# Embedding gathers of chunks 1 to 3: a wait ahead of every two gathers in place of every eight

## The chip, the core and the metric

The kernel runs on one core of a Trainium2 chip. The time is device microseconds (us) of that core for one launch, lower is better. Everything is float32. The engines are TensorE (PE; its weight loads are shown apart as PEld), VectorE (DVE), ScalarE (ACT), GpSimd (POOL) and the queue engine SyncE (SP).

## What is computed

A recommendation tower over a batch of 2048. For each of 32 fields one row of 64 numbers is looked up in that field's own table; for every pair of fields a bilinear product with a 64x64 kernel gives one number; the 496 numbers go through a small network.

```python
e = jnp.stack([tbl_0[ids[:, 0]], ..., tbl_31[ids[:, 31]]], axis=1)   # (2048, 32, 64)
rows, cols = np.triu_indices(32, k=1)                                # 496 pairs
p, q = e[:, rows, :], e[:, cols, :]
pij = jnp.einsum('bpe,dpe,bpd->bp', p, kernel, q)
z = pij @ W.T + b
h = jnp.concatenate([z, dense_ctx], axis=1)
h = jnp.maximum(h @ W_top1 + b_top1, 0.0)
h = jnp.maximum(h @ W_top2 + b_top2, 0.0)
y = h @ W_top3
```

## The kernel before

The batch is cut into 4 chunks of 4 tiles of 128 rows (512 samples). Two fields lie side by side on the 128 partitions and are called a double; there are 16, numbered j = 0 to 15.

**Gathers.** GpSimd fetches the table rows with indirect DMAs, one for each field and tile: 128 rows of 64 floats, 32 KB. A double of one chunk is 2 fields x 4 tiles = 8 gathers. Doubles 3 to 6 go into `emb_first`, which has a buffer for odd and one for even chunks; the others go into `emb`, which has one. For chunk 0 the gathers are issued as early as their order allows (the first six fields are not gathered there but looked up by matmuls). For chunks 1 to 3 they are issued while the chunk before is worked on, and paced: ahead of the 8 gathers of a double stands one wait on `s_bilinear`, the count of slots that TensorE has finished. Its threshold is 40 + 4.6 x ((i - 1) x 16 + j) for chunk i and double j. A wait on the buffer's last reader stands there too (`turned(i - 1, j)`, or the batches of two chunks before).

**Turning.** For chunks 1 to 3 SyncE writes a gathered double of `emb` to HBM and reads it back so that 32x32 blocks lie where VectorE's block transpose (`turn_squares`, L675) can finish the turn into `emb_t`. Doubles 3 to 6 are turned by TensorE (`turn`, L745) and copied by ScalarE. The doubles 0 to 2 of the next chunk are turned at slots 80 to 84 of a chunk's 92, those in `emb_first` at slots 86 and 90, doubles 7 to 15 at slots 8 to 58 of their own chunk.

**Pairs.** A slot (`slot`, L773) multiplies one double with the kernels of another double on TensorE, in 32-column tiles of the array: 8 matmul calls, 16 MATMUL instructions. VectorE multiplies the result in PSUM with the other double (`multiply`, L654). 32 batches a chunk (`batch`, L787) do the same with the operands' roles changed; VectorE multiplies (L665) and ScalarE sums along the row (`reduce`, L584). The products of the slots are summed over partitions by more matmuls (`sum_quad`, L816), the sums of the batches join them (`join`, L799), and the network's layers (`layer_terms`, L859) follow. The results of slots and batches stand in a ring of three pairs of PSUM banks: TensorE can be three units ahead of VectorE.

**Order.** The order of all steps is fixed ahead, in the list `PROGRAM`, that TensorE, VectorE and ScalarE walk through; semaphores tie them. GpSimd has its own loop over chunks and doubles; so has SyncE.

Of the kernel before, what the change touches and what calls it, by code (L numbers as in the profile page):

```python
# [17 lines left out]
DOUBLES = NUM_FIELDS // 2  # L18
# [87 lines left out]

GATHER_LEAD, LEAD_FROM = 3, 7
GATHER_FROM, GATHER_EVERY = 40, 4.6

# [176 lines left out]
def build(nc, moved, tables, ids, looked_ids, dense_t, k_slots, w_cols, l0_b, w_top1, b_top1, w_top2, b_top2, w_top3, out):  # L288
# [6 lines left out]
    with ExitStack() as ctx:  # L295
# [6 lines left out]
        def sem(name):  # L302
            return ctx.enter_context(nc.semaphore(name))
# [64 lines left out]
        s_bilinear = sem("s_bilinear")  # L368
# [15 lines left out]
        def gathered(i, j):  # L384

            if j in BATCH_DOUBLES:
                return (s_gathered_first[i % 2][BATCH_DOUBLES.index(j)],
                        sum(32 * tiles for _, tiles in CHUNKS[i % 2:i + 1:2]))
            first = CHUNKS[1][0] if j < LOOKED_UP else 0
            return s_gathered[OTHER_DOUBLES.index(j)], 32 * (CHUNKS[i][0] + CHUNKS[i][1] - first)  # L390
# [10 lines left out]
        def turned(i, j):  # L401

            if i == 0 and j < LOOKED_UP:
                return s_looked_up, (j + 1) * TABLE_STEPS
            if i > 0 and j not in BATCH_DOUBLES:
                return s_squares, SQUARES_USE[i, j] + 1
            return s_turned, TURN_OF[i, j] - LOOKED_UP + 1

        def fields_of(i, j, t):

            if j in BATCH_DOUBLES:
                at = 2 * BATCH_DOUBLES.index(j)
                return emb_first[:, i % 2, t, at:at + 2, :]
            return emb[:, OTHER_DOUBLES.index(j), t, :, :]
# [58 lines left out]
        @block.gpsimd  # L473
        def _(pool):
            nc.gpsimd.iota(rows_i32[:], pattern=[[1, TABLE_STEPS]], base=0,
                           channel_multiplier=TABLE_STEPS).then_inc(s_rows, 1)
            pool.wait_ge(s_ids[0], 16)
            for i, (start, tiles) in enumerate(CHUNKS):
                if i == 1:
                    pool.wait_ge(s_consts, 1)  # L480
                    pool.wait_ge(s_ids[1], 16)

                    pool.wait_ge(s_one_hot, LOOKED_UP * TABLE_STEPS)
                for j in range(LOOKED_UP if i == 0 else 0, DOUBLES):
                    if i > 0:
                        pool.wait_ge(s_bilinear, int(GATHER_FROM + GATHER_EVERY * ((i - 1) * DOUBLES + j)))
                    elif j >= LEAD_FROM:
                        pool.wait_ge(*turned(0, j - GATHER_LEAD))
                    if j not in BATCH_DOUBLES:

                        if i > (1 if j < LOOKED_UP else 0):
                            pool.wait_ge(*turned(i - 1, j))
                    elif i > 1:

                        pool.wait_ge(*turned(i - 2, j))
                        pool.wait_ge(s_batch_prod, BATCHES_TO[i - 1])
                    for f in (2 * j, 2 * j + 1):
                        for t in range(tiles):
                            nc.gpsimd.indirect_dma_start(  # L499
                                fields_of(i, j, t)[:, f % 2, :], None, tables[f],  # L500
                                bass.IndirectOffsetOnAxis(ap=ids_sb[:, start + t, f:f + 1].bitcast(u32), axis=0),
                            ).then_inc(gathered(i, j)[0], 16)
                    if i == 0 and j == LOOKED_UP:
                        pool.wait_ge(s_consts, 1)
                        nc.gpsimd.affine_select(out=ident[:], in_=ident[:], compare_op=ALU.not_equal, fill=1.0,
                                                base=0, pattern=[[-1, P]], channel_multiplier=1).then_inc(s_ident, 1)
# [427 lines left out]
```

## Time and profile before

| | |
|---|---|
| median of 3 runs | 1318.49 us (1302.54 to 1324.91) |
| profiled execution, its own time | 1308.94 us |
| its span, first to last instruction | 1307.1 us |
| mean granted TensorE clock | 0.867 |
| TensorE matmul busy | 1155.0 us (88%), 11668 instructions |
| VectorE busy | 655.4 us (50%) |
| ScalarE busy | 547.3 us (42%) |
| GpSimd busy | 462.6 us (35%), 488 gathers |
| DMA mean | 38 GB/s |

Busy time counts a matmul from its start to a modelled end, and matmuls overlap: eight 32-column tiles run side by side. So the busy share of TensorE says little; how many MATMUL instructions are done in a microsecond says more. A window view counts an instruction in each window that it touches, so that in windows of 1 us, with matmuls of some 0.6 us, each is counted more than once; over 10 us and more that matters little. PEclk is the granted clock as a share of the full 2.4 GHz.

### The profile page before, as it was taken

The page shows a single profiled execution, that of the slowest core. Times are in us where ns is not written, and L with a number is a line of the kernel's source. Part 1 is how long each engine was busy: PE and PEld are TensorE (multiplying, and loading weights), DVE is VectorE, ACT ScalarE, POOL GpSimd, SP SyncE. Part 2 cuts the span into 40 slices and gives each one's busy share as a digit, 9 for nine tenths or more (in the row PEclk, how much of TensorE's full clock was granted, in tenths as well). Part 3 has the DMA queues.
Part 4 walks back from the last instruction along what each step waited for, and adds up shares of the span by engine and source line. Part 5 has one row for each costly group of instructions (what it writes and reads, how often), then busy time and mean ns, then how long its engine had stood idle before and what let it go on. Part 6 is the DMA issues. An engine that isn't in the chain of part 4 may idle for free.

```text
span 1307.1 us, 29606 instructions
## 1 busy us (share of the span) xinstructions
PE 1155.0 (88%) x11668; PEld 402.8 (31%) x11668; DVE 655.4 (50%) x620; ACT 547.3 (42%) x4163; POOL 462.6 (35%) x494
## 2 busy tenths in 40 slices
PE   5796999679998899998989898998888999999998
PEld 1231423022333224323333232333222333333333
DVE  3261746033445425454444443454444559769990
ACT  0000646124434213543435520235453455469991
POOL 6326242734344444433444444343444420000000
PEclk9796989568778798987779888988988879999999
DMA  7501000220022122012112002200321000400000
GB/s 234 200 11 23 11 17 10 50 40 17 12 49 49 25 58 49 17 28 48 34 41 41 17 18 59 51 16 16 74 57 34 15 12 3 83 2 3 3 3 2
DMA packets 115263, 50.04 MB, mean 38 GB/s; under 512 B 85362, under 2 KB 104562, under 8 KB 114612
## 3 DMA queue, kind: packets, MB, share of 16 engines
q1 hardware_dynamic: 97048, 28.99, 9.2%
q0 software_dynamic: 15616, 16.02, 6.3%
q10 hardware_dynamic: 2460, 3.15, 0.8%
q8 instruction: 91, 1.49, 0.5%
q14 instruction: 48, 0.39, 0.1%
HBM read 38.67 MB, written 9.45 MB: 37 GB/s over the span
## 4 chain that ended last, share of the span: by engine, by line
PE 80%; issue 11%; DVE 6%; another core or an unknown queue 1%; DMA 1%; ACT 0%; DVEq 0%; SPq 0%
PE bilinear L773 39%; PE sums L816 16%; PE bilinear L787 13%; PE bilinear L859 7%; PE bilinear L700 3%; DVE prod L654 3%; PE sums L799 1%; DVE prod L651 1%; DVE batch_prod L665 1%; PE bilinear L745 1%; DMA sums_sb<-looked_ids 1%; DVE w_comb_sb L634 1%; DVE emb_t L675 0%; PE bilinear L710 0%
## 5 line engine op out<-in xcount | busy, mean ns | idle before, releaser
L773 PE MATMUL bilinear<-emb_t,k_sb 64*32 64x512 f32 x5888 | 681.8, 654 | 59.5 <-issue 48.8
L584 ACT ACTIVATE batch_prod<-batch_prod 128x64 f32<-128x64 f32 x2048 | 490.8, 243 | 383.5 <-DVE batch_prod L665 311.9
L654 DVE TENSOR_TENSOR prod<-bilinear,emb_t 128x1024 f32<-128x1024 f32 x352 | 419.4, 1218 | 376.5 <-remote 256.2
L499 POOL DMA_INDIRECT emb<-table,ids_sb x360 | 339.7, 943 | 459.0 <-PE bilinear L773 258.9
L584 ACT ACTIVATION_READ_ACCUMULATOR batch_prod<-batch_prod 128x1 f32 x2048 | 386.9, 189 | 9.6 <-issue 9.1
L816 PE MATMUL sums<-prod,row_sel 64*32 64x512 f32 x2944 | 353.3, 651 | 21.5 <-issue 16.5
L773 PEld LDWEIGHTS bilinear<-emb_t,k_sb 64*32 64x32 f32 x5888 | 189.7, 113 | 432.0 <-issue 382.8
L787 PE MATMUL bilinear<-k_sb,emb_t 64*32 64x512 f32 x2048 | 264.3, 648 | 37.0 <-issue 29.3
L665 DVE TENSOR_TENSOR batch_prod<-bilinear,emb_first 128x1024 f32<-128x1024 f32 x128 | 155.9, 1218 | 177.6 <-remote 155.3
L499 POOL DMA_INDIRECT emb_first<-table,ids_sb x128 | 122.3, 955 | 143.8 <-PE bilinear L773 104.4
L816 PEld LDWEIGHTS sums<-prod,row_sel 64*32 64x32 f32 x2944 | 99.7, 115 | 159.8 <-issue 145.8
L787 PEld LDWEIGHTS bilinear<-k_sb,emb_t 64*32 64x32 f32 x2048 | 70.9, 113 | 156.7 <-issue 137.9
L700 PE MATMUL bilinear<-prod,batch_prod 125*32 125x512 f32 x192 | 41.4, 708 | 22.2 <-issue 11.3
L859 PE MATMUL bilinear<-sums_sb,w_comb_sb 128*128 128x512 f32 x128 | 59.6, 621 | 0.0
L543 ACT ACTIVATE emb_t<-bilinear 128x512 f32<-128x512 f32 (+1 forms) x22 | 15.7, 714 | 98.5 <-PE bilinear L745 72.2
L651 DVE TENSOR_TENSOR prod<-bilinear,emb_t 64x512 f32<-64x512 f32 x64 | 44.1, 689 | 19.9 <-remote 17.2
L565 ACT ACTIVATE h_sb<-bilinear,b_comb_sb 128x512 f32<-128x512 f32 x16 | 11.0, 687 | 94.6 <-PE bilinear L859 89.1
L554 ACT ACTIVATE sums_sb<-sums 128x512 f32<-128x512 f32 x16 | 8.7, 595 | 81.6 <-PE sums L799 52.6
L859 PEld LDWEIGHTS bilinear<-sums_sb,w_comb_sb 128*128 128x128 f32 x128 | 25.0, 200 | 35.9 <-issue 33.1
L620 DVE TENSOR_SCALAR prod<-sums_sb,rows_sb 128x1024 f32<-128x1024 int32 x16 | 12.1, 793 | 38.3 <-remote 19.3
L859 PE MATMUL bilinear<-h_sb,w_sb 128*128 128x512 f32 x64 | 28.4, 597 | 0.0
L700 PEld LDWEIGHTS bilinear<-prod,batch_prod 125*32 125x32 f32 x192 | 9.7, 123 | 52.9 <-issue 41.4
(34 smaller groups left out, 138.8 us busy)
## 6 DMA issues: line engine op xcount, KB each, us to landing
moved<-emb SPq DMA_DIRECT2D x36, 256.0 KB
emb<-moved SPq DMA_DIRECT2D x144, 64.0 KB, 2.1
emb<-table,ids_sb POOLq DMA_INDIRECT x360
emb_first<-table,ids_sb POOLq DMA_INDIRECT x128
k_sb<-k_slots SPq DMA_DIRECT2D x2, 896.0 KB
k_sb<-k_slots SPq DMA_DIRECT2D x1, 1600.0 KB
batch_prod<-table ACTq DMA_DIRECT2D x6, 250.0 KB
k_sb<-k_slots SPq DMA_DIRECT2D x1, 1408.0 KB
```

What stands on the lines that cost most here:

```text
L499: nc.gpsimd.indirect_dma_start(fields_of(i, j, t)[:, f % 2, :], None, tables[f], bass.IndirectOffsetOnAxis(ap=ids_sb[:, start + t, f:f + 1 ...
L543: nc.scalar.activation(emb_t[:, j:j + several, 0:n], bilinear[:, bank:bank + several, 0:n], ACT.Copy).then_inc(s_emb_t, 1)
L584: last = nc.scalar.activation(products, products, ACT.Copy, accum_out=batch_sums[:, t, half, row + f:row + f + 1])
L634: last = nc.vector.tensor_copy(w_comb_sb[rows, g, :], fold_bank(at + 1)[rows, :])
L651: last = nc.vector.tensor_tensor(prod[rows, at + half, 0:n], bilinear[rows, bank + half, 0:n], emb_t[by, double, 0:n], ALU.mult)
L654: last = nc.vector.tensor_tensor(prod[:, at:at + 2, 0:n], bilinear[:, bank:bank + 2, 0:n], emb_t[:, j:j + 1, 0:n].to_broadcast([P, 2, n]), ...
L665: nc.vector.tensor_tensor(batch_prod[:, use % BATCH_PRODS, :, :], bilinear[:, bank:bank + 2, :], first.to_broadcast([P, 2, COLS]), ALU.mul ...
L700: last = nc.tensor.matmul(bilinear[col:col + QUARTER, bank, :], tables_sb[0:TABLE_PARTS, f, k, e:e + QUARTER], one_hot[0:TABLE_PARTS, n % ...
L773: last = nc.tensor.matmul(bilinear[col:col + QUARTER, bank + row // EMB, 0:n], k_sb[row:row + EMB, operand, col:col + QUARTER], emb_t[row: ...
L787: last = nc.tensor.matmul(bilinear[col:col + QUARTER, bank + row // EMB, :], emb_t[row:row + EMB, m, t * P + col:t * P + col + QUARTER], k ...
L816: last = nc.tensor.matmul(sums[32 * b:32 * b + 32, half, 0:n], row_sel[rows, 31 - pos:63 - pos], prod[rows, at + b, 0:n], start=pos == 0, ...
L859: last = nc.tensor.matmul(layer_bank(i, k)[0:weights.shape[1], 0:n], weights, x, start=term == 0, stop=term == LAYER_TERMS[k] - 1)
```

## The change

The one wait on `s_bilinear` ahead of a double's 8 gathers goes. In its place, for chunks 1 to 3, a wait stands ahead of every second gather, with the fraction of the double that is done in its threshold. The thresholds rise by 4.6 x 2 / 8 = 1.15 slots from one to the next. The first two gathers of a double have the threshold of before, the last two one that is 3.45 slots later. That makes 192 waits where there were 48. The number, order, size and place of the gathers stay, and so does everything on the other engines.

```diff
 GATHER_LEAD, LEAD_FROM = 3, 7
 GATHER_FROM, GATHER_EVERY = 40, 4.6
+GATHERS_AT_ONCE = 2
...
                 for j in range(LOOKED_UP if i == 0 else 0, DOUBLES):
-                    if i > 0:
-                        pool.wait_ge(s_bilinear, int(GATHER_FROM + GATHER_EVERY * ((i - 1) * DOUBLES + j)))
-                    elif j >= LEAD_FROM:
+                    if i == 0 and j >= LEAD_FROM:
                         pool.wait_ge(*turned(0, j - GATHER_LEAD))
...
                     for f in (2 * j, 2 * j + 1):
                         for t in range(tiles):
+                            if i > 0 and t % GATHERS_AT_ONCE == 0:
+                                pool.wait_ge(s_bilinear, int(GATHER_FROM + GATHER_EVERY * (
+                                    (i - 1) * DOUBLES + (f * tiles + t) / (2 * tiles))))
                             nc.gpsimd.indirect_dma_start(
```

On GpSimd, where chunk 1 begins (`table_31` is the last of chunk 0; `table_1` and `table_9` are double 0, `table_12` opens double 1; what an instruction waits for stands in brackets), the order before is

```order
L499 DMA emb<-table_31,ids_sb 128x64 x4
L499 DMA emb<-table_1,ids_sb 128x64 [waits s_one_hot,s_bilinear,s_ids1,s_consts]
L499 DMA emb<-table_1,ids_sb 128x64 x3
L499 DMA emb<-table_9,ids_sb 128x64 x4
L499 DMA emb<-table_12,ids_sb 128x64 [waits s_bilinear]
L499 DMA emb<-table_12,ids_sb 128x64 x3
```

and after the change

```order
L501 DMA emb<-table_31,ids_sb 128x64 x4
L501 DMA emb<-table_1,ids_sb 128x64 [waits s_one_hot,s_bilinear,s_ids1,s_consts]
L501 DMA emb<-table_1,ids_sb 128x64
L501 DMA emb<-table_1,ids_sb 128x64 [waits s_bilinear]
L501 DMA emb<-table_1,ids_sb 128x64
L501 DMA emb<-table_9,ids_sb 128x64 [waits s_bilinear]
L501 DMA emb<-table_9,ids_sb 128x64
L501 DMA emb<-table_9,ids_sb 128x64 [waits s_bilinear]
L501 DMA emb<-table_9,ids_sb 128x64
L501 DMA emb<-table_12,ids_sb 128x64 [waits s_bilinear]
```

No gather has moved past another; the run of eight behind one wait has become four pairs, each behind a wait of its own.

Later in chunk 1, where a double of `emb` also waits for its buffer (`table_8` ends double 6, `table_10` and `table_11` are double 7), the order after the change is

```order
L501 DMA emb_first<-table_8,ids_sb 128x64
L501 DMA emb<-table_10,ids_sb 128x64 [waits s_bilinear,s_turned]
L501 DMA emb<-table_10,ids_sb 128x64
L501 DMA emb<-table_10,ids_sb 128x64 [waits s_bilinear]
L501 DMA emb<-table_10,ids_sb 128x64
L501 DMA emb<-table_11,ids_sb 128x64 [waits s_bilinear]
```

The wait for the buffer stays with the first gather of the double; only the waits on the count of slots are new.

## Rows read from the trace of the kernel before

**Rows 1.** Groups of instructions: line, engine; busy us, mean ns; idle before and releaser.

```profile
...
L773 PE MATMUL bilinear<-emb_t,k_sb 64*32 64x512 f32 x5888 | 681.8, 654 | 59.5 <-issue 48.8 <-DVE prod L651 3.0 <-DVE prod L654 0.8
...
L654 DVE TENSOR_TENSOR prod<-bilinear,emb_t 128x1024 f32<-128x1024 f32 x352 | 419.4, 1218 | 376.5 <-remote 256.2 <-PE bilinear L773 88.0 <-issue 31.4
...
L499 POOL DMA_INDIRECT emb<-table,ids_sb x360 | 339.7, 943 | 459.0 <-PE bilinear L773 258.9 <-PE bilinear L745 102.4 <-issue 97.2
...
L675 DVE STREAM_TRANSPOSE emb_t<-emb 128x512 f32<-128x512 f32 x36 | 25.3, 702 | 0.2
```

**Rows 2.** Windows of two long stretches: us busy and instructions by engine.

```profile
...
core 0: us, PE busy (x) PEld busy (x) DVE busy (x) ACT busy (x) POOL busy (x), PEclk, DMA share, GB/s
276.00:1066.00 790.00, 705.92 (x6409) 247.15 (x6394) 357.36 (x327) 317.41 (x2415) 339.63 (x360) 0.85 0.17 35
1070.00:1262.00 192.00, 190.41 (x3096) 70.30 (x3088) 169.01 (x160) 140.82 (x1115) 0.00 (x0) 1.00 0.08 16
```

**Rows 3.** Timeline of GpSimd's gathers: start, duration, idle before.

```profile
...
654.86 0.94 POOL L499 DMA_INDIRECT emb<-table,ids_sb  x1 [9.27 <-PE bilinear L773]
...
663.60 0.94 POOL L499 DMA_INDIRECT emb<-table,ids_sb  x1 [0.30 <-issue]
671.96 0.94 POOL L499 DMA_INDIRECT emb<-table,ids_sb  x1 [7.42 <-PE bilinear L773]
```

**Rows 4.** Windows of 0.5 us at a burst's start; columns as in Rows 2.

```profile
...
656.00:656.50 0.50, 0.50 (x17) 0.38 (x11) 0.50 (x2) 0.50 (x6) 0.40 (x1) 1.00 0.00 0
656.50:657.00 0.50, 0.50 (x18) 0.20 (x5) 0.50 (x1) 0.50 (x6) 0.50 (x1) 1.00 0.42 66
657.00:657.50 0.50, 0.50 (x12) 0.04 (x3) 0.50 (x2) 0.50 (x7) 0.20 (x2) 1.00 0.05 16
657.50:658.00 0.50, 0.50 (x5) 0.12 (x2) 0.44 (x1) 0.50 (x6) 0.50 (x1) 1.00 0.37 66
```

**Rows 5.** Windows of 1 us at that burst's end.

```profile
...
665.00:666.00 1.00, 1.00 (x5) 0.12 (x1) 0.00 (x0) 0.00 (x0) 0.00 (x0) 0.50 0.19 33
666.00:667.00 1.00, 1.00 (x10) 0.46 (x15) 0.69 (x1) 0.00 (x0) 0.00 (x0) 0.50 0.00 0
```

**Rows 6.** Windows of its held stretch and of the climb behind it.

```profile
...
657.50:666.20 8.70, 7.79 (x22) 1.37 (x20) 0.44 (x1) 1.52 (x13) 5.52 (x6) 0.72 0.14 26
666.20:669.00 2.80, 2.80 (x41) 1.64 (x46) 2.69 (x3) 1.43 (x12) 0.00 (x0) 0.64 0.32 94
```

**Rows 7.** Timeline of TensorE's weight loads inside that burst.

```profile
...
664.06 0.12 PEld L773 LDWEIGHTS bilinear<-emb_t,k_sb 64*32 64x32 f32 x1 [0.54 <-issue]
664.77 0.18 PEld L773 LDWEIGHTS bilinear<-emb_t,k_sb 64*32 64x32 f32 x3 [0.59 <-issue]
```

**Rows 8.** Timeline of VectorE behind that burst.

```profile
...
657.24 0.70 DVE L675 STREAM_TRANSPOSE emb_t<-emb 128x512 f32<-128x512 f32 x1
666.31 1.23 DVE L665 TENSOR_TENSOR batch_prod<-bilinear,emb_first 128x1024 f32<-128x1024 f32 x1 [8.37 <-remote]
```

**Rows 9.** Windows of 2 us inside another burst, launched at 915.2 to 923.9.

```profile
...
911.00:913.00 2.00, 2.00 (x49) 0.87 (x36) 1.41 (x2) 2.00 (x18) 0.00 (x0) 1.00 0.00 0
...
919.00:921.00 2.00, 1.23 (x4) 0.36 (x5) 0.00 (x0) 0.05 (x1) 1.70 (x2) 1.00 0.17 33
...
925.00:927.00 2.00, 1.64 (x11) 0.48 (x19) 0.11 (x1) 0.61 (x6) 0.00 (x0) 1.00 0.10 16
```

**Rows 10.** Timeline of TensorE in the longest burst, 32 gathers from 227.4 us.

```profile
...
248.51 1.01 PE L787 MATMUL bilinear<-k_sb,emb_t 64*32 64x512 f32 x1 [0.39 <-issue]
...
260.41 1.01 PE L787 MATMUL bilinear<-k_sb,emb_t 64*32 64x512 f32 x1 [1.78 <-issue]
```

**Rows 11.** Timeline of TensorE, the last chunk's join.

```profile
...
1278.77 3.26 PE L799 MATMUL sums<-ident,batch_sums 128*32 128x128 f32 x64
```

**Rows 12.** Windows of 10 us in the last chunk, without gathers.

```profile
...
1230.00:1240.00 10.00, 10.00 (x197) 3.69 (x192) 10.00 (x9) 8.11 (x62) 0.00 (x0) 1.00 0.01 2
```

## Prediction, made before the changed kernel was run

> **What bounds the kernel now.** I read the groups of instructions first. VectorE's main product takes 1218 ns each time and VectorE is idle for 376 us before those of L654; GpSimd is idle before its gathers for 459 us in `emb` alone; no engine is full by its own work [rows 1]. So I compared two long stretches with and without gathers. From 276 to 1066 us, with 360 gathers (45 bursts of 8), TensorE does 6409 MATMUL instructions in 790 us, 8.1 a microsecond; from 1070 to 1262 us, with none, it does 3096 in 192 us, 16.1 a microsecond, at a granted clock of 1.00 against 0.85 [rows 2]. The program is much the same in both. One burst and what follows it take 790 / 45 = 17.56 us and hold 6409 / 45 = 142 instructions, which the stretch without gathers would do in 142 / 16.1 = 8.8 us. The gathers therefore cost 17.56 - 8.8 = 8.7 us per burst, 45 x 8.7 = 394 us in all. That is the sum this change works on.
>
> Next, one burst. The 8 launches start at 654.86 and end with the one at 663.60, so (663.60 - 654.86) / 7 = 1.25 us each; the next burst starts at 671.96 [rows 3]. Gather traffic shows in the half microsecond from 656.5 (none in the one before), 1.64 us after the first launch or a little less; TensorE goes on at 17 or 18 instructions per half microsecond to 657.0, has 12 in the next and 5 in the one from 657.5 [rows 4] (such short windows count a matmul twice; what matters is the fall). The traffic is still there in the window 665 to 666 and gone in the next, in which TensorE comes back [rows 5]. VectorE, done at 657.94, gets its next product at 666.31 [rows 8]. So TensorE is held from some 2.5 us after the first launch (the lead-in) to 666.2, which is 2.6 us after the last one (the wake): 8.7 us with 22 instructions, 2.5 a microsecond [rows 6]. Inside, weight loads come 0.71 us apart, with the releaser "issue", so no semaphore holds them [rows 7]. VectorE waits for TensorE, not for a port; its product takes 1218 ns in and out of bursts. What holds TensorE the profile doesn't name; it goes with the gathers' traffic. The hold deepens with length: late in the burst of 32, a matmul every 1 to 2 us [rows 10].
>
> **The change, part by part.** The 192 waits cost GpSimd nothing that matters: it is idle 7.4 us before each burst [rows 3]. Behind a wait on GpSimd stand only later gathers. They come up to 3.45 slots (3.45 x 17.56 / 4.6 = 13 us) later. Doubles are fetched far ahead: for chunk 1, the last pair of double 15 goes at slot 112.45 instead of 109 and is turned at slot 92 + 58 = 150; of double 6, at slot 71 instead of 67 and turned at slot 90. SyncE's move through HBM waits for a whole double and stands in order behind earlier moves; VectorE's turns at its end wait 0.2 us in all now [rows 1]. With 19 slots to spare at the closest (some 70 us), lateness costs nothing; if that cover were gone, it would be at most 13 us for each of 3 chunks.
>
> What changes is the hold. For n launches in a row it is 1.25 x (n - 1) + 2.6 - lead-in; for n = 8 and a lead-in of 2.5, 8.8, as seen. For n = 2 the trace has no case, and it all turns on how much of the lead-in comes back ahead of each pair. Ends, per 8 gathers (4 pairs):
> - the whole lead-in of 2.5 us: 4 x 1.35 = 5.4 us held;
> - only the 1.6 us before the traffic starts, in which nothing can hold TensorE yet: 4 x 2.25 = 9.0 us held;
> - none, so that the pair holds from its launch on: 4 x 3.85 = 15.4 us.
>
> The second is nearest to the rows. The 0.9 us between traffic and fall is work handed to TensorE ahead of time, and to have it again TensorE's supply would have to run ahead of its work. The fastest that instructions come in this trace is 64 of 128 columns in 3.26 us, 19.6 a microsecond [rows 11], and TensorE at full work takes 19.7 a microsecond [rows 12]; no row shows supply faster than work. Now to the time. In the hold 2.5 instructions a microsecond get done. With 9.0 us held, 142 - 22 = 120 are left: at 19.7 a microsecond 6.1 us, so 15.1 us for 8 gathers; at the 16.1 of the long stretch, 7.5 us, so 16.5 us. The lower end holds if TensorE catches up at its best rate after each short hold, since VectorE has up to three units in PSUM to live on; the upper if it doesn't. I take 15.7, the middle. The same way of counting gives for now 8.7 + 120 / 16.1 = 16.2, 1.4 us under the 17.56 of the trace; part of that is the climb after a hold, 2.8 us at a mean clock of 0.64 with 41 instructions [rows 6], which takes 2.8 - 41 / 16.1 = 0.3 us. A hold of 2 us should leave the clock up: in another burst TensorE does 4 instructions in 919 to 921, and the clock is still 1.00 in 925 to 927 [rows 9]; in the one above, a mean of 0.72 over the hold puts the fall from 1.00 to 0.50 some 3.8 us into it [rows 6]. So 17.56 - 15.7 = 1.9 us saved per 8 gathers, x 45 = 84 us. The gathers before 276 us and the last chunk stay as they are.
>
> The profiled execution took 1308.94 us by itself: 1308.94 - 84 = 1225 us. The median of the runs is 9.6 us above that execution, so the same kernel would measure up to 1235; I state 1230.
>
> At this point a rule of the Trainium skill bears on the lead-in. The row shows work going on for 0.5 to 1 us after the first traffic [rows 4]. "TensorE: Matmul & The Clock Gate", in its part on the array of 32x32 pieces, gives TensorE a queue of 64 instructions, in which loads are pulled ahead. A full queue would be 32 pairs of load and matmul, an estimate of 1.6 us at 19.7 a microsecond, so the lead-in would be the queue running dry. With a queue that is full again at each pair the first end above would hold, and the sum would be 1122 us; by the rows on supply it isn't, and the sum is 1225.
>
> **The rivals.**
> - *The lead-in comes back whole.* 5.4 us held, 13 instructions in it, 129 left at 16.1: 8.0 + 5.4 = 13.4 us, 4.2 saved, x 45 = 187 us: 1122 us. For it: TensorE waits now and then for VectorE, which is busy 10.00 of 10 us in the fast stretch [rows 12], and it may then run ahead. Against it: the supply rate. Chance 0.15.
> - *The hold goes by gathers, not by bursts.* Each gather holds TensorE for 8.7 / 8 = 1.1 us wherever it stands; pacing changes nothing but the clock's climb. That gives between 1309 and 1309 - 45 x 1.4 (all that the count above leaves open) = 1246, most likely near 1290. For it: lead-in and wake are nearly equal (2.5 and 2.6 us), so a burst looks like one hold moved in time. Chance 0.22. The skill's page "SBUF — State Buffer" (on its two separate sides) leads to the same outcome by another way: a DMA "cannot be slowed by a compute op, and vice versa". By it the traffic doesn't hold TensorE and splitting it brings nothing; the trace disagrees, with 8.1 against 16.1 instructions a microsecond [rows 2], but shows only that the two go together. It has 0.05 of this case's 0.22.
> - *Slower: the clock stays at its lower level.* Now TensorE has some 9 us of unbroken work between holds. With pairs it works and stands in turns of about 2 us, and the climb may never come. At half of 19.7, 9.9 a microsecond, 142 instructions take 14.4 us. Holds of 5.4 to 9.0 us come on top, less 2.5 a microsecond of work in them (1.4 to 2.3 us): 18.4 to 21.1 us for 8 gathers, +0.8 to +3.5, x 45 = +38 to +160 us: 1347 to 1466 us. It decides from the point at which the clock is at the lower level for over half of the stretch. For it: the clock already falls within a burst (mean 0.72 over the hold, 0.64 behind it [rows 6]). Against it: it stays at 1.00 through most of a hold of 8 us [rows 9]. Chance 0.12. The page on TensorE says that the throttled state is the default and that sustained activity lifts it, which points the same way.
> - *Slower: each pair pays from its launch.* 15.4 us held, 39 instructions in it, 103 left: 6.4 + 15.4 = 21.8, +4.2 x 45 = +191: 1500 us. Against it: TensorE works at full rate for 2 us after the launch [rows 4]. Chance 0.06.
>
> That the change doesn't do what it says, because TensorE passes the thresholds faster than GpSimd serves them and the pairs close up into a long burst, would need 1.15 slots in under 2.5 us; at full pace they take 8.8 / 4 = 2.2 us, but with any hold at all more. It regulates itself, and falls under the second rival.
>
> **How the numbers follow.** Forecast 0.45 (15.1 to 16.5 us per 8 gathers: 1198 to 1261 us), lead-in whole 0.15, by gathers 0.22, clock 0.12, from the launch 0.06. The range leaves out the two slower ones (0.18) and reaches from below the lead-in case, 1100, to the top of the runs of before, 1325. Two per cent, 26 us, is about what a measurement of this kernel can tell from no change. Faster by over that: 0.43 of the forecast, 0.15, and 0.05 of the third: 0.63. Within: 0.02 + 0.17 = 0.19. Slower: 0.18.
>
> **What the changed profile would show.** 45 x 4 pairs with GpSimd idle 1 to 2 us before each; TensorE at about 142 / 15.7 = 9.0 instructions a microsecond in the gather stretch; a granted clock near 1.0 there; VectorE's idle time before L654 shorter. A clock near 0.5 to 0.7 would mean the first slower rival; 8.1 a microsecond the third case; over 10 the whole lead-in. The prediction is wrong if a short hold differs in kind from a long one, which no row of before can show.

## The result, and the profile after

The changed kernel takes 1144.73 us (median of 4 runs, 1141.08 to 1149.14) against 1311.7 us of before in the same series: a ratio of 0.875, 95% interval 0.867 to 0.883. It is faster by 167 us; 84 us were forecast. The span of the profiled execution is 1143.7 us, its mean granted clock 0.939 against 0.867.

The groups of instructions after the change (the lines have moved down by two), answering to [rows 1]:

```profile
...
L775 PE MATMUL bilinear<-emb_t,k_sb 64*32 64x512 f32 x5888 | 594.0, 617 | 44.3 <-issue 30.2 <-DVE prod L656 3.0 <-DVE prod L653 1.5
...
L656 DVE TENSOR_TENSOR prod<-bilinear,emb_t 128x1024 f32<-128x1024 f32 x352 | 418.8, 1216 | 265.9 <-remote 158.8 <-PE bilinear L775 105.1 <-issue 0.8
...
L501 POOL DMA_INDIRECT emb<-table,ids_sb x360 | 340.1, 945 | 346.1 <-PE bilinear L775 129.3 <-PE bilinear L747 89.8 <-issue 83.0
...
L677 DVE STREAM_TRANSPOSE emb_t<-emb 128x512 f32<-128x512 f32 x36 | 25.2, 701 | 0.2
```

VectorE's product and GpSimd's gather take as long as before (1216 and 945 ns); TensorE's matmul of L775 reads 617 ns instead of 654, with an end that is modelled. What has changed is the idle time: VectorE's before L656 went from 376.5 to 265.9 us, GpSimd's before the gathers into `emb` from 459.0 to 346.1. The block transposes at the end of the gathers' path (L677) wait 0.2 us in all, as before: the gathers' lateness reached nobody.

The long stretches, answering to [rows 2]; the first now holds 364 gathers:

```profile
...
257.00:910.00 653.00, 600.73 (x6505) 218.22 (x6505) 362.92 (x333) 319.63 (x2463) 343.91 (x364) 0.97 0.22 43
920.00:1095.00 175.00, 173.37 (x2796) 61.91 (x2796) 153.14 (x147) 125.89 (x991) 0.00 (x0) 1.00 0.09 18
```

TensorE does 6505 / 653 = 10.0 instructions a microsecond beside the gathers, where it did 8.1, and 16.0 without them, as before. For 8 gathers the stretch takes 653 / 45.5 = 14.4 us, where it took 17.56 and 15.7 were forecast. So 3.2 us x 45.5 = 146 us of the 163 between the two spans were won here. The rest lies ahead of it: the first spaced gathers start at 257.6 us instead of 276.2. Of these 18.6 us, 9.5 were there before any changed instruction ran, so they are not the change's (the long run of gathers that ends chunk 0 starts at 217.9 us instead of 227.4; in the traces of the experiments below it starts between 208 and 228 us); that run has 28 gathers now instead of 32.

GpSimd's launches, two pairs and a four (start, duration, idle before), answering to [rows 3]:

```profile
...
311.86 0.95 POOL L501 DMA_INDIRECT emb_first<-table,ids_sb  x1 [1.18 <-PE bilinear L775]
313.11 0.94 POOL L501 DMA_INDIRECT emb_first<-table,ids_sb  x1 [0.30 <-issue]
315.04 0.95 POOL L501 DMA_INDIRECT emb_first<-table,ids_sb  x1 [0.99 <-PE bilinear L775]
...
318.87 0.94 POOL L501 DMA_INDIRECT emb<-table,ids_sb  x1 [1.63 <-PE bilinear L775]
320.11 0.94 POOL L501 DMA_INDIRECT emb<-table,ids_sb  x1 [0.30 <-issue]
321.36 0.95 POOL L501 DMA_INDIRECT emb<-table,ids_sb  x1 [0.30 <-issue]
322.61 0.94 POOL L501 DMA_INDIRECT emb<-table,ids_sb  x1 [0.30 <-issue]
```

The gathers at 318.87 and 321.36 belong to two pairs; by the time the first was launched TensorE had passed the second's threshold, and they closed up. Counting all launches after 255 us that follow each other within 1.4 us as one burst, the trace has 48 pairs, 55 fours and 8 sixes.

Windows of 0.5 us around the pair launched at 311.86 (columns as in [rows 4]):

```profile
...
312.50:313.00 0.50, 0.50 (x21) 0.25 (x9) 0.50 (x2) 0.50 (x5) 0.31 (x1) 1.00 0.00 0
...
313.50:314.00 0.50, 0.50 (x15) 0.04 (x2) 0.50 (x1) 0.50 (x6) 0.50 (x1) 1.00 0.34 66
314.00:314.50 0.50, 0.50 (x9) 0.11 (x3) 0.05 (x1) 0.50 (x6) 0.05 (x1) 1.00 0.00 0
314.50:315.00 0.50, 0.50 (x11) 0.27 (x15) 0.13 (x1) 0.50 (x6) 0.00 (x0) 1.00 0.29 62
315.00:315.50 0.50, 0.50 (x17) 0.23 (x5) 0.50 (x1) 0.50 (x7) 0.46 (x1) 1.00 0.02 4
```

From 21 instructions TensorE falls to 15, then to 9 and 11 from 314.0 to 315.0, and is back at 17 half a microsecond later: its lowest window starts 2.1 us after the pair's first launch, and a short, shallow dip is all. Windows of 1 us over the four launched from 318.87 to 322.61:

```profile
...
320.00:321.00 1.00, 1.00 (x25) 0.20 (x16) 1.00 (x2) 1.00 (x11) 0.89 (x1) 1.00 0.20 33
321.00:322.00 1.00, 0.98 (x22) 0.23 (x11) 0.53 (x1) 1.00 (x10) 0.69 (x2) 1.00 0.15 33
322.00:323.00 1.00, 0.69 (x11) 0.00 (x0) 0.00 (x0) 1.00 (x10) 0.69 (x2) 1.00 0.01 0
323.00:324.00 1.00, 0.62 (x2) 0.23 (x3) 0.00 (x0) 0.23 (x2) 0.56 (x1) 1.00 0.15 33
324.00:325.00 1.00, 0.44 (x9) 0.29 (x16) 0.34 (x1) 0.00 (x0) 0.00 (x1) 1.00 0.20 33
325.00:326.00 1.00, 1.00 (x26) 0.29 (x15) 1.00 (x2) 0.08 (x1) 0.94 (x1) 1.00 0.00 0
```

Here it falls to 11, 2 and 9 a window, from 322, 3.1 us after the first launch, to 325, 2.4 us after the last. The clock is 1.00 throughout; behind the burst of eight it was at 0.50 and climbed [rows 6]. The two timelines tell more closely when TensorE comes back, here and behind the burst of eight of before:

```profile
...
324.56 0.62 PE L775 MATMUL bilinear<-emb_t,k_sb 64*32 64x512 f32 x2 [0.81 <-issue]
...
666.26 1.07 PE L816 MATMUL sums<-prod,row_sel 64*32 64x512 f32 x2
```

That is 1.95 us after the last launch (322.61) and 2.66 us after it (663.60).

### The profile page after: what moved, and what is told of

It is laid out like the page before. It is cut to its first block, busy times and chain, and to the rows that moved or that the text cites. A ratio compares the mean times of both kernels' runs of the same rounds, so it can differ in the third digit from the quotient of the medians.

```text
span 1143.7 us, 29606 instructions
## 1 busy us (share of the span) xinstructions
PE 1035.1 (91%) x11668; PEld 365.4 (32%) x11668; DVE 653.4 (57%) x620; ACT 543.7 (48%) x4163; POOL 466.5 (41%) x494
## 3 DMA queue, kind: packets, MB, share of 16 engines
q0 software_dynamic: 15616, 16.02, 7.1%
## 4 chain that ended last, share of the span: by engine, by line
PE 81%; issue 10%; DVE 6%; another core or an unknown queue 1%; DMA 0%; ACT 0%; DVEq 0%
PE bilinear L775 39%; PE sums L818 15%; PE bilinear L789 14%; PE bilinear L861 8%; DVE prod L656 3%; PE bilinear L702 3%; DVE prod L653 1%; DVE batch_prod L667 1%; PE sums L801 1%; PE bilinear L747 1%; PE bilinear L717 1%; DMA batch_prod<-table 0%; PE sums L717 0%; PE bilinear L712 0%
## 5 line engine op out<-in xcount | busy, mean ns | idle before, releaser
L775 PE MATMUL bilinear<-emb_t,k_sb 64*32 64x512 f32 x5888 | 594.0, 617 | 44.3 <-issue 30.2
L656 DVE TENSOR_TENSOR prod<-bilinear,emb_t 128x1024 f32<-128x1024 f32 x352 | 418.8, 1216 | 265.9 <-remote 158.8
L501 POOL DMA_INDIRECT emb<-table,ids_sb x360 | 340.1, 945 | 346.1 <-PE bilinear L775 129.3
L818 PE MATMUL sums<-prod,row_sel 64*32 64x512 f32 x2944 | 294.3, 614 | 7.2 <-issue 4.4
L775 PEld LDWEIGHTS bilinear<-emb_t,k_sb 64*32 64x32 f32 x5888 | 161.8, 108 | 370.0 <-issue 306.0
L789 PE MATMUL bilinear<-k_sb,emb_t 64*32 64x512 f32 x2048 | 236.0, 606 | 31.9 <-issue 28.6
L667 DVE TENSOR_TENSOR batch_prod<-bilinear,emb_first 128x1024 f32<-128x1024 f32 x128 | 155.7, 1216 | 140.4 <-remote 126.2
L501 POOL DMA_INDIRECT emb_first<-table,ids_sb x128 | 125.8, 983 | 96.3 <-PE bilinear L775 42.4
L818 PEld LDWEIGHTS sums<-prod,row_sel 64*32 64x32 f32 x2944 | 91.8, 110 | 120.6 <-issue 101.3
L789 PEld LDWEIGHTS bilinear<-k_sb,emb_t 64*32 64x32 f32 x2048 | 57.9, 107 | 156.3 <-issue 123.6
L545 ACT ACTIVATE emb_t<-bilinear 128x512 f32<-128x512 f32 (+1 forms) x22 | 15.7, 713 | 97.9 <-PE bilinear L747 45.8
L861 PE MATMUL bilinear<-sums_sb,w_comb_sb 128*128 128x512 f32 x128 | 56.8, 598 | 0.0
L702 PE MATMUL bilinear<-prod,batch_prod 125*32 125x512 f32 x192 | 32.5, 642 | 11.5 <-issue 11.1
L556 ACT ACTIVATE sums_sb<-sums 128x512 f32<-128x512 f32 x16 | 8.7, 594 | 64.6 <-PE sums L801 45.5
L677 DVE STREAM_TRANSPOSE emb_t<-emb 128x512 f32<-128x512 f32 x36 | 25.2, 701 | 0.2
```

The source lines that it names most:

```text
L501: nc.gpsimd.indirect_dma_start(fields_of(i, j, t)[:, f % 2, :], None, tables[f], bass.IndirectOffsetOnAxis(ap=ids_sb[:, start + t, f:f + 1 ...
L545: nc.scalar.activation(emb_t[:, j:j + several, 0:n], bilinear[:, bank:bank + several, 0:n], ACT.Copy).then_inc(s_emb_t, 1)
L656: last = nc.vector.tensor_tensor(prod[:, at:at + 2, 0:n], bilinear[:, bank:bank + 2, 0:n], emb_t[:, j:j + 1, 0:n].to_broadcast([P, 2, n]), ...
L667: nc.vector.tensor_tensor(batch_prod[:, use % BATCH_PRODS, :, :], bilinear[:, bank:bank + 2, :], first.to_broadcast([P, 2, COLS]), ALU.mul ...
L677: nc.vector.transpose(emb_t[:, j, :], emb[:, at, :, :, :].rearrange("p t f e -> p (t f e)")).then_inc(s_squares, 1)
L702: last = nc.tensor.matmul(bilinear[col:col + QUARTER, bank, :], tables_sb[0:TABLE_PARTS, f, k, e:e + QUARTER], one_hot[0:TABLE_PARTS, n % ...
```

## The experiments

The first four kernels, and that of e15, put one question: how the cost goes with the number of gathers in a row. Each is shown with the window over its gather stretch (columns as in [rows 2]); a table behind e15 puts them side by side. The five series fell on five chips, which turned out to matter: e1 to e4 ran on the first, e5 to e8 on the second. On which chip the two kernels of the result ran is not on record.

**e1_four.** The changed kernel with steps of four.

```diff
-GATHERS_AT_ONCE = 2
+GATHERS_AT_ONCE = 4
```

> Gathers in steps of four, thresholds spread in the same way. Theory L (the lead-in comes back): every burst gives TensorE its first 2.5 us free, so n launches in a row hold it for 1.25 x (n - 1) + 0.1 us; twice 3.85 = 7.7 us per 8 gathers against 5.4 for pairs and 8.8 for eights, which puts the time between the two kernels: 1200 to 1240 us. Theory G (the hold goes by gathers, and what the pairs won is the clock): four launches hold TensorE for 4 us or so, in which the clock doesn't fall either, so the time is that of pairs, 1140 to 1165 us.

1160.9 us (1160.43 to 1169.09), ratio 0.8985 (0.8888 to 0.9082): 39 us below L's range and within G's. The bursts are 82 fours and 4 eights. Most of the gain comes with the first halving, which is the number that G gives and not the one of L. L was priced from the holds alone; what it leaves out is taken up below. G falls by the next kernels. The stretch:

```profile
...
258.00:925.00 667.00, 608.65 (x6474) 218.88 (x6459) 358.77 (x331) 318.53 (x2452) 339.57 (x360) 0.97 0.21 41
```

**e2_one.** Steps of one.

```diff
-GATHERS_AT_ONCE = 2
+GATHERS_AT_ONCE = 1
```

> Gathers one at a time, a wait ahead of each, 0.575 slots apart. Theory L: a lone launch holds TensorE for 0.1 us, but 0.575 slots are 1.1 us of TensorE's work at full pace and a launch takes 1.25 us, so many close up; 1050 to 1110 us, and clearly below the pairs. Theory G: as the pairs, 1135 to 1155 us. A third theory, that the waits themselves or a shallower fill of the lead-in cost: above 1155 us.

1114.96 us (1112.74 to 1120.09), ratio 0.8623 (0.8532 to 0.8714). That is 46 us less than e1_four in the same series, where G has all sizes of step take the same time, and 5 us above the range of L. The pairs of the result were 30 us slower, but in another series, and the two ratios' intervals overlap (0.853 to 0.871, 0.867 to 0.883). The bursts after 255 us are 12 ones, 36 twos, 37 threes, 28 fours and 10 longer.

```profile
...
259.00:880.00 621.00, 577.64 (x6456) 217.82 (x6448) 359.81 (x331) 314.32 (x2431) 338.52 (x359) 0.98 0.23 45
```

**e3_late.** The kernel before with all thresholds 1.7 slots later.

```diff
-GATHER_FROM, GATHER_EVERY = 40, 4.6
+GATHER_FROM, GATHER_EVERY = 41.7, 4.6
```

> The kernel before, eights behind one wait, with every threshold 1.7 slots later: the mean lateness of the change without its splitting. L and G: no difference from before, within 1%. If the lateness itself brought the gain (gathers meeting other work), 1145 to 1250 us.

1323.11 us (1313.14 to 1338.19), ratio 1.019 (1.004 to 1.034): being late brings no gain. It was expected to be within 1%; the interval leaves open whether it costs anything worth naming.

```profile
...
269.00:1080.00 811.00, 732.57 (x6360) 239.38 (x6345) 354.75 (x326) 317.93 (x2423) 339.67 (x360) 0.83 0.17 34
```

**e4_wide.** The changed kernel with thresholds further apart.

```diff
-GATHER_FROM, GATHER_EVERY = 40, 4.6
+GATHER_FROM, GATHER_EVERY = 40, 5.3
```

> Pairs as in the changed kernel, thresholds 1.325 slots apart in place of 1.15 (GATHER_EVERY 5.3). At 1.15 slots TensorE passes a threshold in about 2.2 us at full pace while two launches take 2.5 us, and the trace shows some pairs closed up into fours and sixes. L: fewer closed-up pairs, 13.4 to 14 us per 8 gathers in place of 14.4, 1105 to 1130 us. G: 1140 to 1150 us, as now.

1101.82 us (1093.57 to 1109.29), ratio 0.851 (0.841 to 0.862). 84 pairs now stay pairs, 46 are fours, 2 sixes. G's 1140 to 1150 us is out. The gain over the pairs of the changed kernel is 43 us (another series; the ratios' intervals, up to 0.862 and from 0.867, stand apart). L gave the direction, for fewer closed-up pairs, and too little: the time is 3 us below its range. With 5.3 the gathers reach over more slots, so the stretch has more instructions.

```profile
...
255.00:930.00 675.00, 632.46 (x7517) 235.52 (x7509) 414.07 (x384) 345.87 (x2667) 343.38 (x364) 0.98 0.23 45
```

**e8_one_wide.** Both: steps of one and 5.3.

```diff
-GATHER_FROM, GATHER_EVERY = 40, 4.6
-GATHERS_AT_ONCE = 2
+GATHER_FROM, GATHER_EVERY = 40, 5.3
+GATHERS_AT_ONCE = 1
```

> Gathers one at a time and thresholds spread wider (GATHER_EVERY 5.3): the two steps that won by themselves. By the sum over bursts (1.25 x (n - 1) + 0.1 us each) more lone launches and fewer threes and fours: 1065 to 1090 us. If the gain of smaller steps is used up by the launches closing up, no better than the wide pairs, 1095 to 1105 us.

808.32 us, and the kernel before 809.38 us in the same series: ratio 0.9986 (0.9977 to 0.9996). The series ran on another chip, and there the whole phenomenon is missing. In e8's trace, a stretch with 259 gathers and the one behind it with 5:

```profile
...
310.00:640.00 330.00, 326.38 (x5456) 115.82 (x5443) 296.07 (x280) 249.53 (x1982) 244.98 (x259) 1.00 0.33 66
640.00:780.00 140.00, 137.82 (x2276) 47.76 (x2260) 127.56 (x120) 119.70 (x971) 4.73 (x5) 1.00 0.05 10
```

TensorE does 5456 / 330 = 16.5 instructions a microsecond beside 259 gathers and 16.3 behind them. TensorE passes the thresholds faster than GpSimd serves them, and up to 138 launches follow each other within 1.4 us each; by the rule of the other chips such a run would hold it throughout. On this chip nothing holds it, so there is nothing for pacing to win.

**e5_narrow, e6_plain, e7_act** were to tell what holds TensorE, and fell on that same chip. All three start from the kernel before; all leave out the lookup of chunks 2 and 3, e5 in part. e5 fetches a quarter of each row:

```diff
-                                fields_of(i, j, t)[:, f % 2, :], None, tables[f],
+                                fields_of(i, j, t)[:, f % 2, 0:width], None,
+                                tables[f].rearrange("n (a e) -> (n a) e", e=width),
```

with `width` 16 for chunks 2 and 3. e6 has a plain DMA on GpSimd's queue there:

```diff
+                            if i > 1:
+                                nc.gpsimd.dma_start(
+                                    fields_of(i, j, t)[:, f % 2, :], tables[f][0:P, :]).then_inc(gathered(i, j)[0], 16)
+                                continue
```

e7 has the same transfer on ScalarE's queue, two behind each `reduce` step, with semaphores of its own:

```diff
+                if kind == "reduce" and 1 <= i < NCHUNKS - 1:
+                    copy_rows(i + 1)
+                    copy_rows(i + 1)
```

> The kernel before, but the gathers of chunks 2 and 3 fetch a quarter of a row each (16 of 64 floats, from wrong places): as many descriptors and launches, a quarter of the bytes. It leaves out most of the lookup of these chunks. If the bytes on the way hold TensorE, the hold of a burst shrinks from about 8.7 us towards 2 to 4 us and TensorE does 12 or more instructions a microsecond in the stretch of these gathers. If the making or number of descriptors does it, the hold and the 8.1 a microsecond stay.

> The kernel before, but for chunks 2 and 3 GpSimd issues plain DMAs of 128 consecutive table rows in place of the gathers: same queue, same bytes and rows' size, no indices. It leaves out the lookup of these chunks. If it is the gather by indices that holds TensorE (index reads, a descriptor for each row), the hold goes or shrinks with the launches' length; if anything that GpSimd's software queue moves holds it, the bursts look as before, in proportion to how long a launch takes.

> The kernel before, but the transfers of chunks 2 and 3 are plain DMAs of 128 consecutive table rows, issued by ScalarE's hardware queue, two behind each sum of a batch; GpSimd is done after chunk 1. It leaves out the lookup of these chunks. If GpSimd's software queue is what holds TensorE, the stretch of these transfers runs at 15 to 16 instructions a microsecond and the kernel at 1309 - 32 x 8.7 = 1030 us; if the traffic of 128 rows of 256 bytes does it by itself, TensorE is held as before, spread out: 1150 us or more.

808.05, 807.71 and 808.39 us, one execution each: no difference from 809.38, and no answer.

**e9_act_again, e10_narrow_again.** The kernels of e7 and e5 once more.

> The kernel of e7_act once more (before, with the transfers of chunks 2 and 3 as plain DMAs on ScalarE's hardware queue, two behind each sum of a batch; the lookup of these chunks is left out), because the run of e7_act fell on a chip on which the kernel before itself took 809 us and nothing is held. On such a chip: 808 us again. On one where before takes about 1300 us: if GpSimd's software queue is what holds TensorE, 15 to 16 instructions a microsecond in the stretch of these transfers and about 1030 us; if the traffic of 128 rows of 256 bytes does it from any queue, 1150 us or more.

> The kernel of e5_narrow once more (before, with gathers of a quarter of each row in chunks 2 and 3, which leaves out most of their lookup). On a chip where before takes about 810 us: 808 us again. On one where it takes about 1300 us: the bytes as cause give 12 or more instructions a microsecond in the stretch of the narrow gathers and 1100 to 1200 us; descriptors or launches as cause give 8.1 a microsecond and about 1300 us.

A third chip, and a free one too: 808.42 and 808.6 us, before 808.15 us.

**e11_after, e12_act_third.** The changed kernel and that of e7, on a fourth chip.

> The changed kernel itself once more. On a chip where before takes about 1300 us: 0.87 to 0.88 of it, as measured. On one where before takes about 810 us and TensorE isn't held: the splitting has nothing to win, 0.995 to 1.005 of before.

> The kernel of e7_act for the third time (before, with the transfers of chunks 2 and 3 as plain DMAs on ScalarE's hardware queue; their lookup is left out), in the hope of a chip on which TensorE is held. There: 15 to 16 instructions a microsecond and about 1030 us if GpSimd's software queue is the cause, 1150 us or more if the traffic is. On the other kind of chip: 808 us.

Here before took 1308.3 us. e11: 1153.05 us (1143.28 to 1157.95), ratio 0.878 (0.870 to 0.886): the result repeats on another chip of the kind. e12: 1025.09 us in one execution, and in its trace the stretch of the transfers from ScalarE's queue, then the one of the gathers of chunk 1 from GpSimd's:

```profile
...
500.00:850.00 350.00, 346.48 (x5590) 123.57 (x5579) 305.65 (x290) 258.11 (x2019) 0.00 (x0) 1.00 0.29 61
266.00:496.00 230.00, 202.21 (x1804) 64.87 (x1789) 96.24 (x87) 81.64 (x602) 98.36 (x104) 0.85 0.18 36
```

16.0 instructions a microsecond (5590 / 350) beside 61 GB/s, 7.8 (1804 / 230) beside 36 GB/s. The same chip, the same kernel, the same bytes a transfer: more traffic does not hold TensorE. These transfers come two at a time, though, and not in eights; e13 has them in eights.

**e13_plain_again, e14_narrow_third, e15_one_wide_again.** The kernels of e6, e5 and e8, on a fifth chip, where before took 1289.52 us.

> The kernel of e6_plain again (before, with plain DMAs of 128 consecutive rows from GpSimd's queue in place of the gathers of chunks 2 and 3; their lookup is left out). e12 took the queue and the indices away at once and TensorE was free. If the software queue alone holds TensorE, the bursts of plain DMAs hold it too, for as long as the burst lasts, and the kernel takes 1150 to 1310 us; if it is the gather by indices, 1030 us as e12. On a chip where before takes 810 us it tells nothing.

> The kernel of e5_narrow again (before, gathers of a quarter of each row in chunks 2 and 3; most of their lookup is left out). As many launches and descriptors, a quarter of the bytes. Hold by bytes: 12 or more instructions a microsecond there and 1100 to 1200 us. Hold by descriptors or launches: 8.1 and about 1300 us.

> The kernel of e8_one_wide again (one gather at a time, GATHER_EVERY 5.3). On a chip where before takes about 1300 us: 1065 to 1090 us if the shorter bursts add up (e2_one 1115, e4_wide 1102), 1095 to 1105 if the launches close up again.

e13: 1013.98 us in one execution. The stretch of the plain DMAs and that of the gathers ahead of it:

```profile
...
480.00:800.00 320.00, 315.78 (x5011) 111.44 (x5018) 280.02 (x264) 247.36 (x1973) 138.88 (x260) 0.99 0.27 62
270.00:470.00 200.00, 179.97 (x1582) 59.20 (x1573) 85.13 (x77) 70.02 (x515) 83.00 (x88) 0.83 0.17 34
```

15.7 a microsecond against 7.9, on the same queue of the same engine. GpSimd is busy 535 ns for a plain DMA and 943 ns for a gather:

```profile
...
L503 POOL DMA_INDIRECT emb<-table,ids_sb x168 | 158.5, 943 | 200.1 <-PE bilinear L749 79.3 <-PE bilinear L777 73.6 <-issue 46.0
...
L500 POOL DMA_DIRECT2D emb<-table x192 | 101.4, 535 | 111.3 <-PE bilinear L777 106.5 <-issue 4.7
```

The queue moves 15616 packets and 16.02 MB, as in the kernel before, so it isn't their number either. Behind one burst of 8 plain DMAs, launched from 529.92 to 533.80, windows of 1 us show a dent of 1 to 2 us, in which VectorE stays busy:

```profile
...
532.00:533.00 1.00, 1.00 (x32) 0.14 (x22) 1.00 (x2) 1.00 (x11) 1.00 (x3) 1.00 0.20 62
...
535.00:536.00 1.00, 1.00 (x10) 0.17 (x3) 1.00 (x2) 1.00 (x10) 0.00 (x0) 1.00 0.12 33
536.00:537.00 1.00, 1.00 (x3) 0.08 (x1) 0.96 (x2) 1.00 (x10) 0.00 (x0) 1.00 0.00 0
537.00:538.00 1.00, 1.00 (x25) 0.45 (x32) 0.98 (x2) 1.00 (x8) 0.00 (x0) 1.00 0.00 0
```

Averaged over the 32 bursts of 8 plain DMAs there is no dent: in no half microsecond of the 10 us from the first launch does TensorE start fewer than 12 instructions a microsecond. Windows of 1 us in which fewer than 6 start are as rare as without any gathers: 38 of 298 here, 22 of 192 behind the gathers of before, but 385 of 790 beside them. By the rule for gathers, such a burst would hold TensorE for 4.0 us.

e14: 1308.22 us in one execution against 1289.52. Narrow gathers (470 to 1068 us, of which the first 16 gathers are still full ones) and full ones (277 to 470), with the bytes of the queue, which were 16.02 MB before:

```profile
...
470.00:1068.00 598.00, 537.36 (x4866) 187.68 (x4866) 272.79 (x250) 245.19 (x1878) 257.19 (x272) 0.86 0.14 25
277.00:470.00 193.00, 169.07 (x1548) 55.73 (x1533) 85.37 (x77) 71.61 (x536) 83.20 (x88) 0.82 0.17 34
```

```profile
...
q0 software_dynamic: 15616, 9.73, 4.9%
```

8.1 and 8.0 instructions a microsecond, and 8.2 from 506 us on, with the narrow ones alone (4598 in 562 us). A quarter of the bytes holds TensorE as long.

e15: 1078.57 us (1067.92 to 1087.64), ratio 0.838 (0.832 to 0.844), the shortest time on a chip of this kind. It lies in L's range. Before is faster on this chip too, and the ratio's interval touches that of e4_wide (0.841 to 0.862). There are about 40 ones, 40 twos, 70 threes and 7 longer; many launches here follow at 1.40 to 1.45 us, so the count hangs on the limit.

```profile
...
259.00:897.00 638.00, 606.38 (x7394) 234.51 (x7391) 410.04 (x378) 339.83 (x2615) 339.45 (x359) 0.99 0.24 48
```

All sizes of step together: e1 to e4 from one chip, e15 from another, before and after from the series of the result. "Lost" is the length of the gather stretch less its instructions at 16.1 a microsecond, from the windows above and [rows 2]; "rule" is the sum of 1.25 x (n - 1) + 0.1 us (lead-in 2.5, wake 2.6) over the bursts that the trace has:

| kernel | lost, us | rule, us |
|---|---|---|
| before, eights | 392 | 398 |
| e3_late, eights | 416 | 398 |
| e1_four | 265 | 351 |
| after, pairs and closed-up fours | 249 | 327 |
| e2_one | 220 | 309 |
| e4_wide | 208 | 303 |
| e15_one_wide_again | 179 | about 270 |

Among the split ones the loss falls with the rule, about 1.1 us for each of its microseconds (265 - 179 = 86 against 351 - 270 = 81). Between them and the eights lies a step that the rule doesn't have: it would put the eights at 265 + 47 x 1.1 = 317 us, and they lose 75 to 100 more. What it is made of stands under "Where the time was won" below.

## Why the prediction was wrong, step by step

**What bounds the kernel** was right: TensorE is held beside the gathers, and 392 us of before lie there. Also right: no semaphore does it, and VectorE only waits; the turns at the end of the gathers' path still wait 0.2 us in all. A shift alone brought no gain (e3_late); that it cost 1.9% (0.4 to 3.4%) was not expected, and its cause was not looked for. Two slips in the sums change nothing: the middle of 15.1 and 16.5 is 15.8 and not 15.7, and 1309 + 160 is 1469 and not 1466.

**The step that failed** is the hold of a pair. I took 2.25 us, "only the 1.6 us before the traffic starts", because no row showed supply faster than work. The traces show a lead-in before every burst, however short the gap: 1.35 us a pair was the other end, and the pairs stay under even that. In quarters of a microsecond from the first launch, averaged over the 84 pairs of e4_wide, TensorE starts 15 17 14 15 16 12 13 7 13 5 7 25 instructions a microsecond, and over the 48 of the changed kernel it is the same fall and return. It is down for half a microsecond or little more, and back at 2.75 us, 1.5 us after the second launch. Averaged over the 55 fours of the changed kernel, windows of 1 us from the one of the first launch have

```
23 25 19 11 6 4 15 23
```

instructions, and the 82 fours of e1_four 23 25 19 11 7 6 16 24: full work for over two microseconds, bottom from 4 to 6, back at 7. The same for the 45 eights of before is 26 25 19 11 6 4 3 4 5 4 3 8 17 20: the same fall at the same place.

The ground for 2.25 us, that no row shows supply faster than work, was false of the trace of before itself. I had taken the last chunk's join, 64 matmuls of 128 columns in 3.26 us [rows 11]. The same 64 for chunk 2 take 1.96 us:

```profile
...
1107.32 1.96 PE L799 MATMUL sums<-ident,batch_sums 128*32 128x128 f32 x64
```

That is 32.7 instructions a microsecond, well above the 19.7 at which TensorE works off those of 512 columns. So instructions can come faster than TensorE does the pairs' work, and work can be ahead of it again at each burst. That this is how it comes by work for 0.9 us beyond the traffic's start is argued, not shown. The queue of 64 instructions that the Trainium skill gives TensorE ("TensorE: Matmul & The Clock Gate", the part on the 32x32 pieces) would give such a lead-in if it fills between bursts; no run here shows the queue itself.

**The other ends.** Pairs that stayed pairs and held for 1.35 us would by the first rival's sum have given 13.4 us per 8 gathers. Measured were 14.4. I had dismissed closing up: "with any hold at all more" than 2.2 us per threshold was true on average and false behind a hold, where TensorE, with its buffers full, passes two thresholds in the time of one pair. By the rule the mixture of pairs, fours and sixes is 327 / 45.5 = 7.2 us held per 8 gathers: between the 5.4 and the 9.0 of the prediction. e4_wide agrees that this is what cost: fewer fours, less lost. So does e2_one, with 38 bursts of four and more against 63.

**Where the time was won.** In my sum the hold itself was to lose as much as before, 9.0 us per 8 gathers against 8.7 and 2.5 instructions a microsecond in both; all of the 1.9 us were to come from outside it, from work at up to 19.7 instructions a microsecond and from the clock. The traces have it the other way round. Here the stretches are parted by the rule, from 2.5 us after a burst's first launch to 2.6 us after its last, and the MATMUL instructions that start in each part are counted:

| kernel | inside, us | instructions a us | lost inside, us | outside, instructions a us | lost outside, us |
|---|---|---|---|---|---|
| before | 398 | 2.8 | 329 | 13.5 | 63 |
| e1_four | 351 | 6.3 | 214 | 13.5 | 51 |
| after | 327 | 7.3 | 179 | 12.7 | 70 |
| e4_wide | 303 | 9.3 | 128 | 12.6 | 81 |

The whole gain of the changed kernel lies inside, 150 us, and none outside. The 2.5 instructions a microsecond that I gave a short hold are 7.3. Two things make it so. The hold is deeper when it is long: the eights do 3 to 6 instructions a window for seven windows, the fours 4 to 7 for two. And TensorE comes back sooner behind a short burst: at the median 2.60 us after the last launch of an eight (45 bursts, most from 2.55 to 2.64), 1.90 us after that of a four (82 of e1_four, most from 1.85 to 1.99), 1.5 us after that of a pair. The wake of 2.6 us, read from one burst of eight, was mis-sized for short ones, so the rule overprices them. That accounts for most of the step between eights and fours: 115 of the 127 us between before and e1_four lie inside. Why the wake grows was not tested; behind the eights the clock is at 0.50, behind the fours and pairs at 1.00.

**The clock** did stay up, as forecast (0.97 in the stretch). What it gave back can't be seen by itself. In the windows of 1 us outside the holds the trace of before has 127 us at the lower level, that of after 32; at half the rate that would be (127 - 32) / 2 = 47 us, an estimate. But outside the holds as a whole TensorE does 13.5 instructions a microsecond before and 12.7 after, so something else has taken it up; what, was not looked for.

**The rivals.** The hold by gathers alone is out: 359 to 364 gathers in every stretch, and 179 to 416 us lost. The clock staying low is out: mean 0.97 in the stretch. The payment from the launch on is out: it gave 1500 us. The whole lead-in came nearest, 1122 us forecast with a chance of 0.15; the measured time lies between it and the forecast's 1198 to 1261 us.

**What holds TensorE** I had put down as going "with the gathers' traffic". That is refuted in the part that matters: plain transfers of the same size from ScalarE's queue (e12) or GpSimd's own (e13) leave TensorE at 15.7 to 16.0 instructions a microsecond, and gathers with a quarter of the bytes (e14) hold it as full ones do. What is left is what a gather by indices makes GpSimd and its queue do. Whether that is the reading of the indices, the 128 separate row addresses or the longer launch (1.25 us from one to the next against 0.52 to 0.73) was not told apart. Each of e12, e13 and e14 is one execution; the difference in each is read between two stretches of its own trace. Nor was why the chips differ: the kernel before took 1290 to 1310 us on three of the five, 808 to 809 us on two. For plain traffic e12 agrees with the rule of the Trainium skill ("SBUF — State Buffer", its two separate sides): 16.0 instructions a microsecond beside it against 16.1 without in before. Beside the gathers, with 7.8 on the same chip, the measurement goes against the rule as it is worded, and decides.

## What to carry to other kernels

Where an engine stalls beside another's bursts, measure three lengths before splitting them: how long it goes on after the start, how long it stays down after the end, and how fast it recovers; a first part that is free each time is worth more the shorter the burst, and a wake read behind a long burst need not hold behind a short one. Then check that the pacing keeps the short bursts apart when the paced engine sprints, since thresholds closer than a burst's own length close up. And run before and after on more than one chip: here the change is worth 12.5% on one kind, and a stronger form of it 0.1% on the other (e8_one_wide; the changed kernel itself was not run there). Last, read all instances of an operation before one is called the fastest: here another join was 1.7 times as fast, and it bore on the forecast.

## What the runs showed of the hardware

Two kinds of chip. Where before takes 1290 to 1310 us, TensorE does 8 instructions a microsecond beside gathers by indices, on three chips and in the series of the result; where it takes 808 to 809 us, on two chips, it does 16.5 (e8_one_wide; e10_narrow_again, 5441 in 330 us beside narrow gathers). The launches take 0.94 to 0.95 us on both.

A gather of 128 rows of 64 bytes holds TensorE as long as one of 256 bytes. A plain DMA of 128 rows from the same queue takes GpSimd 0.54 us instead of 0.94 and hardly holds it (15.7 instructions a microsecond).

Behind the last gather of a burst TensorE stays held for 1.5 us after a pair, 1.9 after a four and 2.6 after an eight.

In e8_one_wide, on a free chip, another wait comes forward, once 25.3 us, of TensorE for the small DMAs of `dense_t`, which SyncE issues behind the moves of gathered doubles:

```profile
...
PE bilinear L861 <- DMA sums_sb<-dense_t: 25.3, 1, 25.3
```
